# Decoder layer, cross-attention stage: longer distances between the slots' steps, side work spread over the slots, and the second layer norm applied by ACT

## The chip, the cores and the metric

One Trainium2 chip, one NeuronCore. The metric is the device time of one launch in microseconds; lower is better. PE is TensorE, DVE is VectorE, ACT is ScalarE, POOL is GpSimd, SP is SyncE, which here only issues DMAs.

## The reference, cut to what matters

64 sequences of 64 tokens, width 256, so 4,096 token rows. Three sublayers, each followed by a residual add and a layer norm without weights:

```python
x = _layernorm(x + attn(x))            # 16 heads of 128, ALiBi, causal
x = _layernorm(x + xattn(x, ctx, seg)) # the stage that is changed
x = _layernorm(x + ffn(x))             # bit-linear: activations quantised to 8 bits by row

# xattn
kv_c = kv @ W_kvc                      # 64 wide, shared by all heads
q_c = q @ W_dq                         # 96 wide
q_nope, q_rope = q_c @ W_uq, _rope(q_c @ W_qr)
k_nope, v, k_rope = kv_c @ W_uk, kv_c @ W_uv, _rope(kv_c @ W_kr)
scores = (q_nope . k_nope + q_rope . k_rope) * scale
scores = where((k_ids <= seg) & (k_ids >= seg - 8), scores, NEG)
out = softmax(scores) @ v
out @ W_o
```

The kernel folds W_uq with W_uk and W_uv with W_o beforehand, so that keys and values are the 64 latent columns of each token.

## The kernel before, in words

The layer runs as blocks: self-attention, a short start of cross-attention (`start_cross`), cross-attention, feed-forward. Each block ends when all its engines have ended. The change touches only `cross_attention` (lines 816 to 1254).

**Tiling.** The 4,096 tokens are 8 tiles of 512 tokens (8 sequences). The 16 heads are taken two at a time, so a tile has 8 slots and the stage 64 work items m. Line 865: `S_AT, T_AT, PV_AT, PROJ_AT = 3, 4, 6, 7`. In slot n = 8j + g (j the tile, g from 0 to 7) every engine runs a fixed list of steps written out by hand; a step with distance d works on item m = n - d. The loop has 82 slots: 64 with new items and 18 that drain the pipeline. Engines are not in lockstep: each runs its own list in order, and semaphores hold it where data or a buffer is missing.

**Steps of one item**, by short names that the prediction uses:

- R, L (PE, L1002 and L1006, distance 0): rotary part and latent part of the queries, three passes of bf16 high and low parts each. turn, cos (DVE, L1142 and L1156) multiply the rotary part with the tables; SP sends `x_turn` to `x_turned` with two DMAs that swap row pairs (L923); qh (DVE, L1151, distance 1) adds both; lat (ACT, L1086) copies the latent part; qhl (POOL, L793 from L1228, distance 1) makes the low part.
- S (PE, L971 and L979, distance 3): mask and scores into the one PSUM tile `xsP`. ntop (DVE, L1134): negated row maximum. exp (ACT, L1073): 8 exponentials, each with a row sum.
- inv (DVE, L1124), norm (POOL, L1215), T (PE, L1014: transposes into `xptP`), pth (ACT, L1081), all at distance 4; ptl (DVE, L1129) at distance 5.
- O (PE, L992, distance 6): probabilities times values into `xoP`. oA (ACT, L1064) copies it out; SP rearranges it with four DMAs into `oB` (L917).
- oBl (POOL) and P (PE, L1025, distance 7): low part and output projection, summed over the 8 items of a tile in `xprojP`.

**Order in one slot**, before: PE runs S, O, R, L, other, T, P. ACT runs oA, exp, copy_out, pth, lat, first layer norm (LN1), roots. DVE runs inv, ptl, ntop, residual add, turn, qh, cos, extras. POOL runs norm, oBl, qhl, extras. SP issues oB, then x_turned, then others.

**other** (L936 to L963) is one PE step a slot that also uses the PSUM tile `xoP`; what it is depends on g: transposes of x for the next tile (xt, twice), the key product (kv), the key rotation (kr), the query product (qc), the transpose of the latents (tk), and transposes of quantised rows of an earlier tile (xq, twice). It waits until oA of that slot has emptied `xoP` and until the last other was copied out. copy_out (ACT, L1035) empties `xoP` again; for kr, DVE does it (kturn, L1161), then SP moves 64 rows (moved_k, L927) and DVE adds them in slot g = 6 (kadd, L1167).

**Side work of a tile that is done**: residual add (DVE, L1138, g = 7 of the next tile), bn_stats and bn_aggr (DVE, g = 0 and 1, two tiles on), two small root steps (ACT, L1098 and L1100, g = 2), the second layer norm itself (LN2: DVE, L1182, g = 3, four instructions of 128x256), row maximum for the quantisation (DVE, L1186, g = 4), quantisation (POOL, L1247, g = 6) and its transposes xq. LN1 of the tile two ahead is applied by ACT (L601) as scale times x plus shift, in slots g = 1, 3 and 5. In the slots from 64 on, ACT and DVE also quantise the feed-forward weights (L1105, L1110, L1201, L1203).

Of the kernel before, what the change touches and what calls it, by code (L numbers as in the profile page):

```python
# [5 lines left out]
F32 = mybir.dt.float32  # L6
# [5 lines left out]
P = 128  # L12
# [4 lines left out]
TILE = 512  # L17
# [798 lines left out]
def cross_attention(nc, a, X, norm, ident, late, ffn, sem, sb, part):  # L816
# [20 lines left out]
    probs = sb("x_probs", [P, 2, PB, 2, T], F32)  # L837
# [3 lines left out]
    oBl = sb("oBl", [P, 2, TILE], BF16)  # L841
    xs = late["uqT"][:, :, :].rearrange("p h n -> p (h n)")[:, 0:PB * C].rearrange("p (b c) -> p b c", b=PB)
    stats2 = sb("ln2_stats", [P, NB, 6], F32)
# [21 lines left out]
    S_AT, T_AT, PV_AT, PROJ_AT = 3, 4, 6, 7  # L865
    LAST = N + 2 * HP + 2
# [5 lines left out]
    def step(n):  # L872


        j, g = divmod(n, HP)
        kind, c, tile = (("xq", 0, j - 3), ("xq", 1, j - 3), ("xt", 0, j + 1), ("kv", 0, j + 1),
                         ("xt", 1, j + 1), ("kr", 0, j + 1), ("qc", 0, j + 1), ("tk", 0, j + 1))[g]
        return (kind, c, tile) if 0 <= tile < NT and (kind != "xq" or n < LAST) else (None, 0, 0)

# [14 lines left out]
    with nc.Block() as block:  # L894
        @block.sync
        def _(sp):
# [12 lines left out]
            for n in range(LAST):  # L909
                j, g = divmod(n, HP)  # L910
                if has(n, PV_AT):
# [7 lines left out]
                if has(n, 0):  # L919
                    wait(sp, s_turn, n + 1)  # L920
                    wait(sp, s_qh, n - 1)
                    for h in range(2):
                        sp.dma_start(turned[1 - h::2, n % 2, :], turn[h::2, n % 2, :]).then_inc(s_swap[n % 2], 16)  # L923
                if step(n)[0] == "kr":
                    wait(sp, s_kturn, turns_before(n + 1))
                    wait(sp, s_kadd, turns_before(n))
                    sp.dma_start(moved_k[0:R, :], turned_k[R:P, :]).then_inc(s_kmoved, 16)  # L927
                if g == 4 and j + 3 < NT:
                    wait(sp, s_step, steps_before(n))
                    load_ctx(j + 3)  # L930
                if 1 <= n < 4:
                    ffn_weights(n - 1, ("wgT", "wuT", "wdT")[n - 1])

        @block.tensor
        def _(pe):
# [28 lines left out]
            for n in range(LAST):  # L964
                if has(n, S_AT):
# [14 lines left out]
                    last.then_inc(s_s, 1)  # L980
                if has(n, PV_AT):
# [13 lines left out]
                if has(n, 0):  # L995
                    tile, g = divmod(n, HP)
                    wait(pe, s_qcl, tile)
                    qc = high_part(qcf[:, tile % 2, :]), qcl[:, tile % 2, :]
                    rope_w = high_part(qr[:, g * P:(g + 1) * P]), qrl[:, g * P:(g + 1) * P]
                    wait(pe, s_qh, n - 1)  # L1000
                    for i, (u, z) in enumerate(PASSES):
                        last = nc.tensor.matmul(ropeP[n % 2][:, :], rope_w[u], qc[z], start=(i == 0), stop=(i == 2))  # L1002
                    last.then_inc(s_ropeP, 1)
                    wait(pe, s_lat, n)
                    for i, (u, z) in enumerate(PASSES):
                        last = nc.tensor.matmul(latP[:, :], WQ[:, u, g, :], qc[z], start=(i == 0), stop=(i == 2))  # L1006
                    last.then_inc(s_latP, 1)
                other(n)
                if has(n, T_AT):
                    m = n - T_AT  # L1010
                    wait(pe, s_norm, m + 1)
                    wait(pe, s_ptl, m)
                    for b in range(PB):
                        last = nc.tensor.transpose(ptP[:, b * P:(b + 1) * P], probs[:, m % 2, b].rearrange("p q s -> p (q s)"), ident[:, :])  # L1014
                    last.then_inc(s_pt, 1)
                if has(n, PROJ_AT):
# [10 lines left out]
                    last.then_inc(s_proj, 1)  # L1027
                if n == WEIGHTS_AT + 3:
                    wait(pe, late["s_abs"], 3)
                    wait(pe, s_lat, N)  # L1030
                    nc.tensor.matmul(latP[:, 0:3], kept["ones"][:, :], late["w_sums"][:, :], start=True, stop=True).then_inc(s_sum, 1)

        @block.scalar
        def _(act):
# [21 lines left out]
            LN1_BLOCKS = {1: (0,), 3: (1,), 5: (2, 3)}  # L1056

            for n in range(LAST):
                j, g = divmod(n, HP)
                if has(n, PV_AT):  # L1060
# [5 lines left out]
                if has(n, S_AT):  # L1066
                    m = n - S_AT
                    wait(act, s_top, m + 1)
                    wait(act, s_inv, m)
                    wait(act, s_pt, m - 1)  # L1070
                    for b in range(BT):
                        at_ = b % PB * 2 + b // PB
                        last = nc.scalar.activation(probs[:, m % 2, b % PB, b // PB, :], sP[:, b * T:(b + 1) * T], ACT.Exp,  # L1073
                                                    bias=ntop[:, b:b + 1], accum_out=total[:, at_:at_ + 1])
                    last.then_inc(s_exp, 1)
                copy_out(n)
# [5 lines left out]
                if has(n, 0):  # L1082
# [5 lines left out]
                    last.then_inc(s_lat, 1)  # L1088
                if j + 2 < NT and g in LN1_BLOCKS:
                    for b in LN1_BLOCKS[g]:  # L1090
                        last = norm.by_scalar((j + 2) * PB + b)
                    if g == 5:
                        last.then_inc(s_ln1, 1)
                u = j - 2
                if g == 2 and 0 <= u < NT:
                    own = slice(u * PB, (u + 1) * PB)
                    wait(act, s_mom, NB // NT * (u + 1))
                    nc.scalar.activation(rstd2[:, own], moments[:, own, 1], ACT.Ln, bias=norm.eps_col[:, :]).then_inc(s_ln, 1)  # L1098
                    wait(act, s_ln, u + 1)
                    nc.scalar.activation(rstd2[:, own], rstd2[:, own], ACT.Exp, scale=-0.5).then_inc(s_root, 1)  # L1100
# [13 lines left out]
        def _(dve):  # L1114
# [3 lines left out]
            for n in range(LAST):  # L1118
                j, g = divmod(n, HP)
                if has(n, T_AT):  # L1120
                    m = n - T_AT
# [3 lines left out]
                if has(n, T_AT + 1):  # L1125
                    m = n - T_AT - 1
# [81 lines left out]
        def _(pool):  # L1208
            for n in range(LAST):
                j, g = divmod(n, HP)  # L1210
                if has(n, T_AT):
                    m = n - T_AT
                    wait(pool, s_inv, m + 1)
                    p_ = probs[:, m % 2].rearrange("p b q s -> p (b q) s")
# [6 lines left out]
                if has(n, 1):  # L1221
                    m = n - 1
                    wait(pool, s_lat, m + 1)
                    wait(pool, s_qh, m + 1)
                    wait(pool, s_s, m - 2)
                    low_of(nc.gpsimd, qhl[:, m % 3, :], qh[:, m % 3].rearrange("p b i t -> p (b i t)")).then_inc(s_ql, 1)
                t = j + 1
                if g == 0 and 1 <= j < NT:  # L1228
                    wait(pool, s_out, outs_before(n))
# [11 lines left out]
                if g == 6 and 0 <= j - 2 < NT:  # L1241
                    u = j - 2
                    wait(pool, s_xinv, u + 1)
                    wait(pool, s_step, steps_before(HP * (u + 2) + 2) if u >= 1 else 0)
                    for b in range(PB):
                        i = u * PB + b
                        last = nc.gpsimd.tensor_scalar(xs[:, b, :], X[:, i, :], xinv[:, i:i + 1], MAGIC, ALU.mult, ALU.add)  # L1247
                    last.then_inc(s_xs, 1)
                if g == 7 and t < NT:
                    wait(pool, s_out, outs_before(n))  # L1250
                    low_of(nc.gpsimd, qcl[:, t % 2, :], qcf[:, t % 2, :]).then_inc(s_qcl, 1)
                    wait(pool, s_kadd, t)
                    wait(pool, s_s, HP * (t - 1))
                    low_of(nc.gpsimd, kl[:, t % 2, :], kf[:, t % 2, :]).then_inc(s_kl, 1)
# [225 lines left out]
```

## Time and profile before

| | |
|---|---|
| median of 3 runs | 1553.95 us (1551.09 to 1557.82) |
| the profiled execution's own time | 1553.69 us |
| its span, first to last instruction | 1551.9 us |
| mean granted TensorE clock | 0.978 |
| self-attention and start of cross-attention | 0 to about 997 us |
| cross-attention's slots | about 997 to 1421 us |
| feed-forward | about 1422 to 1552 us |
| busy over the span | PE 91%, DVE 78%, ACT 80%, POOL 79% |

One execution was traced, on the one core. A row of the timeline gives start and length of an instruction in us; a row of the windows gives how long each engine was busy in a stretch. Instructions on one engine overlap by about 0.1 us, so the distance from one start to the next start is what an instruction costs its engine, and is a little less than its length. The turn instruction of slot n on DVE (L1142) is used as the mark of a slot: a tile's length is the time from its first turn to the next tile's.

### The profile page before, as it was taken

What the parts mean: (1) busy time and instruction counts of PE and PEld (TensorE: products, weight loads), DVE (VectorE), ACT (ScalarE), POOL (GpSimd) and SP (SyncE); (2) the same over time, 40 slices, a digit from 0 to 9 for tenths busy, and PEclk for the clock granted to TensorE, in tenths of its full rate; (3) what the DMA queues carried; (4) which work ended last, traced back from release to release, by engine and by line L of the source; (5) the groups of instructions that cost most, each with busy time, mean ns of one, the idle gap of its engine ahead of it and who ended that gap; (6) DMA issues with size and microseconds to landing.
All of it is one profiled execution on the core that took longest, in us unless ns stands there. A gap on an engine that the chain in (4) does not pass through costs nothing. (4 is left out here: it accounts for less than half of the span.)

```text
span 1551.9 us, 53900 instructions
## 1 busy us (share of the span) xinstructions
PE 1411.0 (91%) x19782; PEld 1051.1 (68%) x19986; DVE 1213.6 (78%) x2852; ACT 1245.4 (80%) x4006; POOL 1231.9 (79%) x1196
## 2 busy tenths in 40 slices
PE   5898999999999999999999997789999999875997
PEld 3666777777777777777777775456666667652665
DVE  4877787777777777777777787577988889865997
ACT  5877888888888888888888886488888888873786
POOL 5899889889889888988989985377888888752565
PEclk9999999999999999999999998699999999997999
DMA  7600000000000000000000000244333333320011
GB/s 232 182 12 16 16 3 16 17 3 16 16 3 16 16 3 16 16 3 16 16 3 16 3 3 2 73 139 110 104 101 95 102 95 90 90 69 7 15 42 55
DMA packets 58370, 71.66 MB, mean 46 GB/s; under 512 B 14560, under 2 KB 42528, under 8 KB 58112
## 3 DMA queue, kind: packets, MB, share of 16 engines
q1 hardware_dynamic: 58112, 68.22, 15.1%
q8 instruction: 162, 2.65, 0.7%
q14 instruction: 96, 0.79, 0.2%
HBM read 29.39 MB, written 4.19 MB: 22 GB/s over the span
## 5 line engine op out<-in xcount | busy, mean ns | idle before, releaser
L440 DVE SCALAR_TENSOR_TENSOR X<-projP,r,X 128x256 f32<-128x256 f32 x512 | 211.2, 475 | 3.2 <-PE projP L257 3.2
L237 PEld LDWEIGHTS svP<-W,xT 128*128 128x128 bf16 x3072 | 182.2, 98 | 30.3 <-DVE scores L427 0.2
L503 POOL TENSOR_TENSOR y_sql<-y_sq 128x512 bf16<-128x512 f32 x128 | 133.0, 1039 | 78.7 <-ACT y_sq L324 78.4
L237 PE MATMUL svP<-W,xT 128*128 128x128 bf16 x3072 | 192.5, 219 | 0.0
L208 PE MATMUL qkssP<-xT,W 128*128 128x512 bf16 x641 | 161.4, 383 | 33.4 <-issue 20.3
L208 PE MATMUL kP<-xT,W 128*128 128x512 bf16 x768 | 187.0, 380 | 0.0
L257 PE MATMUL projP<-W,y 128*128 128x256 bf16 x1024 | 177.0, 275 | 3.3 <-POOL yl L503 3.2
L793 POOL TENSOR_TENSOR qhl<-qh 128x1024 bf16<-128x1024 f32 x64 | 121.2, 1893 | 65.6 <-issue 47.7
L339 ACT ACTIVATE probs<-scores,ntop 128x64 f32<-128x64 f32 x512 | 170.5, 339 | 2.1 <-DVE ntop L430 2.0
L1073 ACT ACTIVATE x_probs<-xsP,x_ntop 128x64 f32<-128x64 f32 x512 | 152.4, 332 | 14.9 <-DVE x_ntop L1134 14.6
L503 POOL TENSOR_TENSOR k_sql<-k_sq 128x512 bf16<-128x512 f32 x128 | 133.2, 1040 | 22.1 <-ACT k_sq L344 21.4
L257 PE MATMUL projP<-W,yl 128*128 128x256 bf16 x512 | 141.0, 275 | 0.0
L538 POOL TENSOR_TENSOR ql<-q 128x512 bf16<-128x512 f32 x128 | 139.4, 1089 | 0.0
L503 POOL TENSOR_TENSOR q_sql<-q_sq 128x512 bf16<-128x512 f32 x128 | 133.0, 1039 | 6.5 <-ACT q_sq L331 6.5
L208 PEld LDWEIGHTS kP<-xT,W 128*128 128x128 bf16 x768 | 75.2, 98 | 91.3 <-issue 1.0
L541 POOL TENSOR_TENSOR vl<-v 128x512 bf16<-128x512 f32 x128 | 136.4, 1065 | 0.0
L503 POOL TENSOR_TENSOR yl<-y 128x512 bf16<-128x512 f32 x128 | 133.1, 1039 | 0.0
L470 DVE TENSOR_TENSOR ptl<-pyP,pth 128x256 bf16<-128x256 f32 x128 | 54.3, 424 | 96.7 <-ACT pth L358 96.7
L208 PEld LDWEIGHTS qkssP<-xT,W 128*128 128x128 bf16 x768 | 65.0, 98 | 81.7 <-issue 12.7
L453 DVE COPY v<-svP 128x512 f32<-128x512 f32 x128 | 88.4, 690 | 38.9 <-PE svP L237 37.9
L1073 ACT ACTIVATION_READ_ACCUMULATOR x_probs<-xsP,x_ntop 128x1 f32 x512 | 115.0, 226 | 0.0
L427 DVE SCALAR_TENSOR_TENSOR scores<-svP,r,bias 128x64 f32<-128x64 f32 x512 | 110.0, 278 | 4.5
(251 smaller groups left out, 4914.5 us busy)
## 6 DMA issues: line engine op xcount, KB each, us to landing
x_turned<-x_turn SPq DMA_DIRECT2D x128, 128.0 KB, 2.1
oB<-oA SPq DMA_DIRECT2D x256, 64.0 KB, 2.0
w_stage<-in_wqkvp SPq DMA_DIRECT2D x16, 512.0 KB, 3.3
x_stage<-in_xT SPq DMA_DIRECT2D x8, 512.0 KB, 4.1
X<-in_x SPq DMA_DIRECT2D x1, 4096.0 KB, 16.9
x_stage<-in_ctxT SPq DMA_DIRECT2D x8, 512.0 KB, 4.8
out<-X SPq DMA_DIRECT2D x7, 512.0 KB, 3.0
okv<-in_L_xattn_W_o SPq DMA_DIRECT2D x1, 2048.0 KB, 11.6
```

What stands on the lines that cost most here:

```text
L208: last = nc.tensor.matmul(dst[:, :], weight(parity, u, i, c), xT[:, z, c, tok], start=(c == 0 and k == 0), stop=(c == CC - 1 and k == 2))
L237: last = nc.tensor.matmul(svP[:, b * D:(b + 1) * D], xT[:, u, c, t * TILE + b * P:t * TILE + (b + 1) * P], weight(parity, z, 2, c), start= ...
L257: last = nc.tensor.matmul(projP[:, b * C:(b + 1) * C], y_part, W[:, (j - 3) // NT % 2, z, 3 * CC * D:], start=(i == 0), stop=(i == 2))
L339: last = nc.scalar.activation(probs[:, b, :], scores[:, b, :], ACT.Exp, bias=ntop[:, b:b + 1], accum_out=total[:, b:b + 1])
L427: last = nc.vector.scalar_tensor_tensor(scores[:, b, :], svP[:, b * T:(b + 1) * T], r[:, b:b + 1], row, ALU.mult, ALU.add)
L440: last = nc.vector.scalar_tensor_tensor(acc, projP[:, b * C:(b + 1) * C], r[:, PB + b:PB + b + 1], acc, ALU.mult, ALU.add)
L453: nc.vector.tensor_copy(v[:, j % 4, :], svP[:, :]).then_inc(s_ve, 1)
L503: return nc.gpsimd.tensor_tensor(dst[:, :], src[:, :], high(src, slice(None), 0, TILE), ALU.subtract)
L538: nc.gpsimd.tensor_tensor(ql[:, j % 2, :], q[:, j % 2, :], high_of(q, j % 2), ALU.subtract).then_inc(s_ql, 1)
L541: nc.gpsimd.tensor_tensor(vl[:, j % 4, :], v[:, j % 4, :], high_of(v, j % 4), ALU.subtract).then_inc(s_vl, 1)
L793: return eng.tensor_tensor(dst, src, high_part(src), ALU.subtract)
L1073: last = nc.scalar.activation(probs[:, m % 2, b % PB, b // PB, :], sP[:, b * T:(b + 1) * T], ACT.Exp, bias=ntop[:, b:b + 1], accum_out=tot ...
```

## The change

1. Distances: norm and inv stay at 4; T and pth go to 5, ptl to 6, O and oA to 7, oBl and P to 9. `x_probs` gets a third buffer. The loop has 83 slots.
2. Order in a slot. PE: S, R, L, T, O, P, other. ACT: exp, oA, roots, pth, lat, copy_out, LN1, LN2. DVE: as before with the new distances. POOL: norm, oBl, extras, and qhl last. SP: x_turned before oB.
3. Side work: xt moves from g = 2 to g = 0 and xq from g = 0, 1 to g = 1, 2; LN1 goes one block a slot at g = 0 to 3; the residual add goes to g = 1 one tile later; statistics to g = 2 and 3; roots to g = 4; row maximum to g = 7; quantisation to g = 0; low part of the keys to g = 1 and of the values to g = 4.
4. LN2: a DVE instruction of 128x4 at g = 4 makes shift = -mean * rstd, and ACT applies `scale * x + shift` in two instructions at g = 5 and two at g = 6, in place of DVE's four at g = 3.
5. `oBl` now lies in memory that the folded weights no longer need.

```diff
-    probs = sb("x_probs", [P, 2, PB, 2, T], F32)
+    probs = sb("x_probs", [P, 3, PB, 2, T], F32)
-    S_AT, T_AT, PV_AT, PROJ_AT = 3, 4, 6, 7
-    LAST = N + 2 * HP + 2
+    S_AT, NORM_AT, T_AT, PTL_AT, PV_AT, PROJ_AT = 3, 4, 5, 6, 7, 9
+    LAST = N + 2 * HP + 3
...
-        kind, c, tile = (("xq", 0, j - 3), ("xq", 1, j - 3), ("xt", 0, j + 1), ("kv", 0, j + 1),
+        kind, c, tile = (("xt", 0, j + 1), ("xq", 0, j - 3), ("xq", 1, j - 3), ("kv", 0, j + 1),
                          ("xt", 1, j + 1), ("kr", 0, j + 1), ("qc", 0, j + 1), ("tk", 0, j + 1))[g]
...
-            LN1_BLOCKS = {1: (0,), 3: (1,), 5: (2, 3)}
+            LN1_BLOCKS = {0: (0,), 1: (1,), 2: (2,), 3: (3,)}
...
-                    wait(act, s_pt, m - 1)
+                    wait(act, s_pt, m - 2)
...
+                if g in (5, 6) and 0 <= u < NT:
+                    wait(act, s_shift2, u + 1)
+                    for i in range(u * PB + 2 * g - 10, u * PB + 2 * g - 8):
+                        x = X[:, i, :]
+                        last = nc.scalar.activation(x, x, ACT.Identity, bias=shift2[:, i:i + 1], scale=rstd2[:, i:i + 1])
+                    if g == 6:
+                        last.then_inc(s_ln2, 1)
...
-                if g == 7 and 1 <= j <= NT:
-                    acc = X[:, (j - 1) * PB:j * PB, :]
-                    wait(dve, s_proj, HP * j)
+                u = j - 2
+                if g == 1 and 0 <= u < NT:
+                    acc = X[:, u * PB:(u + 1) * PB, :]
+                    wait(dve, s_proj, HP * (u + 1))
...
-                    if g == 3:
+                    if g == 4:
                         wait(dve, s_root, u + 1)
-                        for i in range(own.start, own.stop):
-                            x = X[:, i, :]
-                            last = nc.vector.tensor_scalar(x, x, moments[:, i, 0:1], rstd2[:, i:i + 1], ALU.subtract, ALU.mult)
-                        last.then_inc(s_ln2, 1)
-                    if g == 4:
+                        nc.vector.scalar_tensor_tensor(shift2[:, own], moments[:, own, 0], -1.0, rstd2[:, own], ALU.mult, ALU.mult).then_inc(s_shift2, 1)
+                    if g == 7:
                         wait(dve, s_ln2, u + 1)
                         nc.vector.tensor_reduce(xsc[:, own], X[:, own, :], AX, ALU.max, apply_absolute_value=True).then_inc(s_max, 1)
```

## Rows read from the trace of the kernel before

**Rows 1.** Busy time by engine (us), granted clock, DMA: tiles 1, 4 and 7
```profile
1035.99:1083.56 47.57, 43.57 (x491) 31.91 (x498) 37.27 (x59) 41.84 (x178) 38.16 (x32) 1.00 0.40 105
...
1180.29:1228.61 48.32, 44.85 (x499) 32.58 (x506) 43.00 (x75) 42.42 (x176) 40.52 (x36) 1.00 0.38 102
...
1325.35:1364.14 38.79, 35.84 (x417) 26.02 (x422) 35.84 (x65) 32.66 (x142) 29.56 (x26) 1.00 0.36 97
```
**Rows 2.** Waits in tile 4: total us, times, longest us
```profile
ACT oA L1064 <- PE xoP L992: 3.7, 4, 1.7
...
ACT x_probs L1073 <- DVE x_ntop L1134: 1.8, 3, 1.1
...
PE xropeP L1002 <- POOL qcl L793: 1.0, 1, 1.0
```
**Rows 3.** Timeline of DVE, slots g = 3 and 4 of tile 4: start, length
```profile
1200.06 3.10 DVE L1182 TENSOR_SCALAR X<-X,ln_moments,ln_rstd 128x256 f32<-128x256 f32 x4
...
1204.36 0.67 DVE L1142 TENSOR_TENSOR x_turn<-xropeP,tabs 128x512 f32<-128x512 f32 x1
...
1207.21 1.22 DVE L1186 TENSOR_REDUCE xsc<-X 128x4 f32<-128x1024 f32 x1
...
1208.77 0.18 DVE L1124 RECIPROCAL x_inv<-x_total 128x8 f32<-128x8 f32 x1
...
1209.46 0.68 DVE L1134 TENSOR_REDUCE x_ntop<-xsP 128x8 f32<-128x512 f32 x1
```
**Rows 4.** Timeline of DVE and of POOL at kadd, slot g = 6 of tile 4
```profile
1218.17 1.93 DVE L1167 TENSOR_TENSOR kf<-turned_k,moved_k 64x512 f32<-64x512 f32 x1
...
1217.67 1.89 POOL L793 TENSOR_TENSOR qhl<-qh 128x1024 bf16<-128x1024 f32 x1 [0.48 <-PE xoP L812]
```
**Rows 5.** LN2 over the stage: ns min/median/max, first and last start
```profile
L1182 DVE TENSOR_SCALAR X<-X,ln_moments,ln_rstd x32: 399/403/1412, 1103.3 to 1412.3; 128x256 f32<-128x256 f32 x32
```
**Rows 6.** Timeline of ACT, slot g = 1 of tile 4
```profile
1186.03 0.31 ACT L1073 ACTIVATE x_probs<-xsP,x_ntop 128x64 f32<-128x64 f32 x1
...
1188.33 0.64 ACT L1041 ACTIVATE xqT<-xoP 128x512 bf16<-128x512 f32 x1
...
1189.29 1.22 ACT L1086 ACTIVATE qh<-xlatP 64x512 f32<-64x512 f32 x2
1190.41 0.59 ACT L601 ACTIVATE X<-X,ln_shift,ln_rstd 128x256 f32<-128x256 f32 x1
1191.01 0.60 ACT L1064 ACTIVATE oA<-xoP 128x512 f32<-128x512 f32 x1
```
**Rows 7.** Timeline at handovers: S on PE, ntop on DVE, exp on ACT
```profile
1194.72 0.38 PE L971 MATMUL xsP<-mask,identb 128*128 128x512 bf16 x1
...
1195.85 0.69 DVE L1134 TENSOR_REDUCE x_ntop<-xsP 128x8 f32<-128x512 f32 x1 [0.18 <-PE xsP L979]
...
1210.17 0.31 ACT L1073 ACTIVATE x_probs<-xsP,x_ntop 128x64 f32<-128x64 f32 x1 [0.59 <-DVE x_ntop L1134]
```
**Rows 8.** Timeline of PE: other (xq, kv, kr) and the T behind it
```profile
1186.67 0.60 PE L946 MATMUL xoP<-ident,uqT 128*128 128x128 f32 x4
...
1197.74 0.42 PE L802 MATMUL xoP<-x_stage,kvf 128*64 128x512 bf16 x1
...
1199.20 0.44 PE L1014 MATMUL xptP<-ident,x_probs 128*128 128x128 f32 x2
...
1210.10 1.12 PE L955 MATMUL xoP<-kf,wkr 64*128 64x512 f32 x2
```
**Rows 9.** The transfer moved_k, all seven: landing time, min/median/max
```profile
DMA to landing us min/median/max: 2.2/2.2/3.7
```
**Rows 10.** The drain: ACT's last exp, and DVE behind the last residual add
```profile
1381.74 0.47 ACT L1073 ACTIVATE x_probs<-xsP,x_ntop 128x64 f32<-128x64 f32 x1
...
1406.55 1.22 DVE L1201 TENSOR_SCALAR okv<-okv 128x2048 f32<-128x2048 f32 x1
...
1408.95 0.42 DVE L1174 BATCH_NORM_STATS2 ln_stats<-X 128x6 f32<-128x256 f32 x1
```

More of the change, by code:

```diff
@@ L840, in cross_attention @@
     oA, oB = sb("oA", [P, 2, 2, HT], F32), sb("oB", [P, 2, TILE], F32)
-    oBl = sb("oBl", [P, 2, TILE], BF16)
-    xs = late["uqT"][:, :, :].rearrange("p h n -> p (h n)")[:, 0:PB * C].rearrange("p (b c) -> p b c", b=PB)
-    stats2 = sb("ln2_stats", [P, NB, 6], F32)
+    spare = late["uqT"][:, :, :].rearrange("p h n -> p (h n)")
+    xs = spare[:, 0:PB * C].rearrange("p (b c) -> p b c", b=PB)
+    oBl = spare[:, PB * C:PB * C + TILE].bitcast(BF16).rearrange("p (s n) -> p s n", s=2)
+    stats2, shift2 = sb("ln2_stats", [P, NB, 6], F32), sb("ln2_shift", [P, NB], F32)
+    s_shift2 = sem("q_shift")
     moments, rstd2, xinv = sb("ln2_moments", [P, NB, 2], F32), sb("ln2_rstd", [P, NB], F32), sb("xinv", [P, NB], F32)
@@ L910, in _ @@
                 j, g = divmod(n, HP)
+                if has(n, 0):
+                    wait(sp, s_turn, n + 1)
+                    wait(sp, s_qh, n - 1)
+                    for h in range(2):
+                        sp.dma_start(turned[1 - h::2, n % 2, :], turn[h::2, n % 2, :]).then_inc(s_swap[n % 2], 16)
                 if has(n, PV_AT):
@@ L918, in _ @@
                                          oA[par * KVC:(par + 1) * KVC, m % 2, i, :]).then_inc(s_ot[m % 2], 16)
[L919 to L923, printed above, removed]
                 if step(n)[0] == "kr":
@@ L980, in _ @@
                     last.then_inc(s_s, 1)
+                if has(n, 0):
+                    tile, g = divmod(n, HP)
+                    wait(pe, s_qcl, tile)
+                    qc = high_part(qcf[:, tile % 2, :]), qcl[:, tile % 2, :]
+                    rope_w = high_part(qr[:, g * P:(g + 1) * P]), qrl[:, g * P:(g + 1) * P]
+                    wait(pe, s_qh, n - 1)
+                    for i, (u, z) in enumerate(PASSES):
+                        last = nc.tensor.matmul(ropeP[n % 2][:, :], rope_w[u], qc[z], start=(i == 0), stop=(i == 2))
+                    last.then_inc(s_ropeP, 1)
+                    wait(pe, s_lat, n)
+                    for i, (u, z) in enumerate(PASSES):
+                        last = nc.tensor.matmul(latP[:, :], WQ[:, u, g, :], qc[z], start=(i == 0), stop=(i == 2))
+                    last.then_inc(s_latP, 1)
+                if has(n, T_AT):
+                    m = n - T_AT
+                    wait(pe, s_norm, m + 1)
+                    wait(pe, s_ptl, m)
+                    for b in range(PB):
+                        last = nc.tensor.transpose(ptP[:, b * P:(b + 1) * P], probs[:, m % 3, b].rearrange("p q s -> p (q s)"), ident[:, :])
+                    last.then_inc(s_pt, 1)
                 if has(n, PV_AT):
@@ L994, in _ @@
                     last.then_inc(s_o, 1)
[L995 to L1015, printed above, removed]
                 if has(n, PROJ_AT):
@@ L1027, in _ @@
                     last.then_inc(s_proj, 1)
+                other(n)
                 if n == WEIGHTS_AT + 3:
@@ L1054, in copy_out @@
                 last.then_inc(s_out, 1)
-            LN1_BLOCKS = {1: (0,), 3: (1,), 5: (2, 3)}
+            LN1_BLOCKS = {0: (0,), 1: (1,), 2: (2,), 3: (3,)}
             for n in range(LAST):
                 j, g = divmod(n, HP)
+                if has(n, S_AT):
+                    m = n - S_AT
+                    wait(act, s_top, m + 1)
+                    wait(act, s_inv, m)
+                    wait(act, s_pt, m - 2)
+                    for b in range(BT):
+                        at_ = b % PB * 2 + b // PB
+                        last = nc.scalar.activation(probs[:, m % 3, b % PB, b // PB, :], sP[:, b * T:(b + 1) * T], ACT.Exp,
+                                                    bias=ntop[:, b:b + 1], accum_out=total[:, at_:at_ + 1])
+                    last.then_inc(s_exp, 1)
                 if has(n, PV_AT):
@@ L1065, in _ @@
                                          ACT.Copy).then_inc(s_oe, 1)
[L1066 to L1069, printed above, removed]
-                    wait(act, s_pt, m - 1)
[L1071 to L1076, printed above, removed]
+                u = j - 2
+                if g == 4 and 0 <= u < NT:
+                    own = slice(u * PB, (u + 1) * PB)
+                    wait(act, s_mom, NB // NT * (u + 1))
+                    nc.scalar.activation(rstd2[:, own], moments[:, own, 1], ACT.Ln, bias=norm.eps_col[:, :]).then_inc(s_ln, 1)
+                    wait(act, s_ln, u + 1)
+                    nc.scalar.activation(rstd2[:, own], rstd2[:, own], ACT.Exp, scale=-0.5).then_inc(s_root, 1)
                 if has(n, T_AT):
@@ L1088, in _ @@
                     last.then_inc(s_lat, 1)
+                copy_out(n)
                 if j + 2 < NT and g in LN1_BLOCKS:
@@ L1091, in _ @@
                         last = norm.by_scalar((j + 2) * PB + b)
-                    if g == 5:
+                    if g == 3:
                         last.then_inc(s_ln1, 1)
[L1094 to L1100, printed above, removed]
+                if g in (5, 6) and 0 <= u < NT:
[5 more added lines that the diff above has]
+                        last.then_inc(s_ln2, 1)
                 k = n - WEIGHTS_AT
@@ L1119, in _ @@
                 j, g = divmod(n, HP)
-                if has(n, T_AT):
-                    m = n - T_AT
+                if has(n, NORM_AT):
+                    m = n - NORM_AT
                     wait(dve, s_exp, m + 1)
@@ L1124, in _ @@
                     nc.vector.reciprocal(inv[:, :], total[:, :]).then_inc(s_inv, 1)
-                if has(n, T_AT + 1):
-                    m = n - T_AT - 1
+                if has(n, PTL_AT):
+                    m = n - PTL_AT
                     wait(dve, s_pth, m + 1)
@@ L1134, in _ @@
                     nc.vector.tensor_reduce(ntop[:, :], by_token(sP[:, :]), AX, ALU.max, negate=True).then_inc(s_top, 1)
-                if g == 7 and 1 <= j <= NT:
-                    acc = X[:, (j - 1) * PB:j * PB, :]
-                    wait(dve, s_proj, HP * j)
+                u = j - 2
+                if g == 1 and 0 <= u < NT:
+                    acc = X[:, u * PB:(u + 1) * PB, :]
+                    wait(dve, s_proj, HP * (u + 1))
                     nc.vector.tensor_tensor(acc, projP[:, :].rearrange("p (b c) -> p b c", b=PB), acc, ALU.add).then_inc(s_acc, 1)
@@ L1210, in _ @@
                 j, g = divmod(n, HP)
-                if has(n, T_AT):
-                    m = n - T_AT
+                if has(n, NORM_AT):
+                    m = n - NORM_AT
                     wait(pool, s_inv, m + 1)
-                    p_ = probs[:, m % 2].rearrange("p b q s -> p (b q) s")
+                    p_ = probs[:, m % 3].rearrange("p b q s -> p (b q) s")
                     nc.gpsimd.tensor_tensor(p_, p_, inv[:, :].unsqueeze(2).to_broadcast([P, BT, T]), ALU.mult).then_inc(s_norm, 1)
@@ L1220, in _ @@
                     low_of(nc.gpsimd, oBl[:, m % 2, :], oB[:, m % 2, :]).then_inc(s_ol, 1)
[L1221 to L1229, printed above, removed]
+                t, u = j + 1, j - 3
+                if g == 0 and 0 <= u < NT:
+                    wait(pool, s_xinv, u + 1)
+                    wait(pool, s_step, steps_before(HP * (u + 2) + 3) if u >= 1 else 0)
+                    for b in range(PB):
+                        i = u * PB + b
+                        last = nc.gpsimd.tensor_scalar(xs[:, b, :], X[:, i, :], xinv[:, i:i + 1], MAGIC, ALU.mult, ALU.add)
+                    last.then_inc(s_xs, 1)
+                if g == 1 and 1 <= j < NT:
+                    wait(pool, s_kadd, j)
+                    wait(pool, s_s, HP * (j - 1))
+                    low_of(nc.gpsimd, kl[:, j % 2, :], kf[:, j % 2, :]).then_inc(s_kl, 1)
+                if g == 4 and 1 <= j < NT:
+                    wait(pool, s_out, outs_before(HP * j))
                     wait(pool, s_o, HP * (j - 1))
@@ L1240, in _ @@
                     low_of(nc.gpsimd, xl[:, c, :], xf[:, c, :]).then_inc(s_xl, 1)
[L1241 to L1248, printed above, removed]
                 if g == 7 and t < NT:
@@ L1251, in _ @@
                     low_of(nc.gpsimd, qcl[:, t % 2, :], qcf[:, t % 2, :]).then_inc(s_qcl, 1)
-                    wait(pool, s_kadd, t)
-                    wait(pool, s_s, HP * (t - 1))
-                    low_of(nc.gpsimd, kl[:, t % 2, :], kf[:, t % 2, :]).then_inc(s_kl, 1)
+                if has(n, 1):
+                    m = n - 1
+                    wait(pool, s_lat, m + 1)
+                    wait(pool, s_qh, m + 1)
+                    wait(pool, s_s, m - 2)
+                    low_of(nc.gpsimd, qhl[:, m % 3, :], qh[:, m % 3].rearrange("p b i t -> p (b i t)")).then_inc(s_ql, 1)
 def ffn_buffers(sb):
```

7 lines of the change are left out of this document (3 added, 4 removed).

## The prediction, made before the changed kernel was run

> **What bounds the stage now.** I read the busy times by stretch first, then the waits inside one tile, then the timeline of that tile. Tiles 2 to 6 repeat to 0.1 us: from the first mark of tile 2 at 1083.56 to that of tile 7 at 1325.35 are 241.8 us, 48.36 each (tile 4 is 48.32) [rows 1]. In tile 4 no engine is full: PE is busy 44.85, DVE 43.00, ACT 42.42, POOL 40.52 [rows 1]. So the tile is bounded by engines that wait for each other while each runs its own list in order. ACT loses 3.7 us waiting for O and 1.8 for ntop; PE loses 1.0 once a tile before R, because qcl is last but one in POOL's list [rows 2]. The long stop is LN2 on DVE: four instructions that took 3.10 us together [rows 3], though the same instruction takes 0.40 in half of its runs and up to 1.41 in others [rows 5]. Behind it stand inv, ptl and ntop, and behind ntop the exponentials: one of ACT's three waits for ntop is 1.1 long [rows 2].
>
> **What one slot costs after the change.** I call t the start of exp on ACT in slot n and ask when the next exp can start. Two things set it.
>
> ACT's own list, by start-to-start distances: exp 2.30 (1186.03 to 1188.33), copy_out and pth together 0.96, lat 1.12, one block of a layer norm 0.60 [rows 6]; oA is 0.60 long with 0.1 of overlap, so 0.50. Sum 5.48 with one norm block, 4.4 bare (without copy_out and norm).
>
> The loop through `xoP`. The new order puts oA behind exp on ACT and other at the end on PE, and other waits for oA: oA ends at t + 2.30 + 0.60, other starts at t + 2.95. S follows other, from S to ntop are 1.13 [rows 7], from ntop to the exp that waits for it 0.71 (1209.46 to 1210.17) [rows 3, 7]. Loop: 4.79 + other. Other is 0.5 for xq and xt (0.60 less overlap), 1.46 for kv (1197.74 to 1199.20), as good as 1.4 for qc, which is six matmuls too, 1.12 for kr [rows 8], about 0.3 for tk.
>
> DVE, when it is late: turn to cos's end 2.85, row maximum with its two small steps 1.56, inv to ntop 0.69, ntop to exp 0.71 [rows 3, 7].
>
> By slot, the larger of them:
> g = 0, 1, 2: ACT 5.5 each (loop 5.3).
> g = 3: loop with kv, 6.25.
> g = 4: ACT with the two roots in place of a norm block, 5.5. The new shift instruction needs the roots, at t + 2.8 + 0.6, and may then stand behind POOL's qhl; I take 5.6.
> g = 5: kr ends at t + 4.07, kturn on DVE 0.6, then 0.69 and 0.71: 6.1 (ACT with two LN2 blocks and no copy_out: 5.6).
> g = 6: loop with qc 6.2; ACT 6.1; DVE with kadd of 1.93 [rows 4], which starts 0.1 before cos ends, 2.75 + 1.93 + 0.69 + 0.71 = 6.1. I take 6.2.
> g = 7: DVE with the row maximum: 2.85 + 1.56 + 0.69 + 0.71 = 5.8.
> Sum 46.45, against 48.36: **1.9 us a tile**.
>
> The shift instruction is not in the trace. Nearest row: kadd, like it with both inputs in SBUF. It starts 0.50 behind a qhl of 1.89 on POOL, and ends 0.54 after it, 1.93 long [rows 4], while turn does the same columns on twice the rows in 0.67 [rows 3]: it seems to have waited for POOL. So the bounds for shift are 0.2 (a 0.18 step on small operands [rows 3]) and 0.2 + 1.9, of which ACT's slack in g = 4 hides little. But qhl starts only behind qh, at about t + 2.15, so it ends at t + 4.05 and shift loses 0.65 at most: the slot is 5.6, not 5.5. The Trainium skill (SBUF — State Buffer, "Who interferes with whom") says that a DVE instruction with two SBUF inputs and a GpSimd instruction that reads SBUF exclude each other for the whole instruction, and that ACT never waits. By that rule shift stands behind any low-part step it meets; if it met a whole qhl, exp in g = 4 would come at t + 6.9 and each tile would be 1.3 longer, some 8 us in all. The kadd row agrees with the rule.
>
> What goes at no cost: LN1 moves are the same 0.60 blocks; T, pth, ptl, O, oBl and P wait for things now one to two slots old (norm, the DMAs into oB), so PE's stops before T and P vanish; qhl as POOL's last step has a whole slot until S needs it; x_turned goes ahead of oB on SP. moved_k is now behind four oB DMAs that wait for oA. It lands in 2.2 to 3.7 [rows 9]; kadd stands a slot later, so I take 0; if it came late, kadd and all behind it would pay. POOL's list stays at 40.5 a tile, under 46.
>
> **The sum.**
> - Fill (slots 0 to 7): 2.0, bounds 0 and 4: no O and oA yet, so no loop; qcl is earlier by a qhl, and kv finds its low parts ready.
> - Tile 1 is 47.57 [rows 1]. No xq, LN2 or maximum after: 5.5 + 5.0 + 5.0 + 6.2 + 5.3 + 6.1 + 6.2 + 5.2 = 44.5: 3.1.
> - Tiles 2 to 6: 5 x 1.9 = 9.5.
> - Tile 7, seven slots, 38.79 [rows 1]: no xt, kv, kr, qc or LN1. 4.7 bare (between ACT's 4.4 and PE's mean of 5.1), 5.4 with the residual add, 5.3, 4.7, 5.3, 5.6, 5.6 = 36.6: 2.2.
> - From 1364.14 to the last exp at 1381.74 [rows 10]: 17.6; after about 17.0: 0.6.
> - Drain: DVE's two weight steps stand between the last residual add and its statistics, 1406.55 to 1408.95 [rows 10]; afterwards they run before that add: 2.4 gained. LN2 there costs 4 x 0.60 on ACT instead of 4 x 0.40 [rows 5, 6] plus shift: 1.0 lost. Net 1.4. The longer distance (P at 9) adds a slot, but drain slots have no work that paces them; ends -2 and +3.
> Together 18.8. Less 1.2 for handovers of 0.03 (ntop's end to exp's start) that my slots leave out: 17.6. The profiled execution took 1553.69 (span 1551.9 and 1.8 around it), the median of the three runs is 1553.95: 1536.
>
> **Rivals.**
> - *PE's floor.* The loop does not close because exp and oA finish earlier than I think. Then a tile is PE's or ACT's busy time: 44.85, or 42.42 + 4 x 0.60 = 44.8. With some waits 45.2: 3.2 a tile for six, 19, and 7 elsewhere: 1527. For it: five of eight slots have only 0.2 between loop and ACT's list. Against: kv, qc and kr are long on PE by themselves. 12%.
> - *Only LN2's stop goes.* The distances change nothing since each stop of PE was absorbed anyway; what goes is the longest wait for ntop, 1.1 [rows 2], seven times: 1546. For it: the waits for O and ntop are ACT's alone and PE is at 93%. 17%.
> - *ACT becomes the bound with its waits kept* (slower). Place: oA, behind exp, with other and copy_out behind it. ACT gets 2.4 more a tile and is then at 44.8, above what any but PE has today. If its idle time stays 5.9 a tile, a tile is 50.7: 7 x 2.4 = 17 more, 1571. It decides from an idle time of 3.6 a tile on; my slots leave 1.7. The Trainium skill (Perfetto Trace Analysis, "Identifying the Most-Contended Engine") says to relieve the engine of highest occupancy first; moving work from DVE to an ACT that thereby becomes fuller than DVE was would by it make a tile 1.8 longer, some 12 us. The trace speaks against it: no engine is full, and ACT's idle time ends at PE and DVE. 8%.
> - Change and gain cancel (the drain takes one more DMA round, moved_k late): 1549. 8%.
>
> **Numbers.** Forecast 55%, its own range 1530 to 1542. The range 1529 to 1547 takes in most of the second rival and leaves out most of the first, the third and the last. About 0.5%, 7.8 us, is what a measurement of this kernel can tell from no change. Faster by more: 0.55 + 0.12 + 0.10 of the second rival = 0.77; within: 0.15; slower: 0.08.
>
> **What would show it.** Tile 4 at 46 to 47 us; its slots g = 3, 5, 6 the longest; no PE wait for qcl and almost none for oBl or norm; a new wait of PE at xt, xq and kv for oA, 0.1 to 0.3 each; ACT busy 44.8 and idle under 2; DVE busy about 40. Wrong if ACT still waits over 3 a tile, if kadd waits for moved_k, if the shift takes over 1 us, or if the drain behind the last exp (40.3 to the end of the stage) grows.

## The result, and the profile of the changed kernel

The changed kernel takes 1538.43 us, median of four runs (1537.75 to 1539.64), against 1554.8 us for the kernel before in the same comparison: a ratio of 0.9896, 95% interval 0.9876 to 0.9916. In a later comparison it took 1539.15 us, ratio 0.9879 (0.9864 to 0.9894). The profiled execution has a span of 1537.0 us against 1551.9. The prediction was 1536, in a range of 1529 to 1547.

Busy time by engine in tiles 1 and 4 after the change (columns as in [rows 1]: PE, PE's weight loads, DVE, ACT, POOL, granted clock, DMA share, GB/s):

```profile
1035.43:1080.31 44.88, 42.12 (x479) 30.69 (x486) 36.33 (x59) 40.81 (x171) 37.21 (x31) 1.00 0.41 110
1172.51:1218.95 46.44, 44.41 (x499) 32.71 (x506) 40.16 (x73) 44.04 (x178) 40.04 (x37) 1.00 0.39 107
```

A tile went from 48.32 [rows 1] to 46.44. ACT is busy for 44.04 of it and idle for 2.4, where it had been idle for 5.9; DVE fell by 2.8. Waits of that tile (total us, times, longest):

```profile
ACT x_probs L1069 <- DVE x_ntop L1143: 1.9, 3, 0.7
...
PEld xoP L952 <- ACT oA L1076: 1.1, 2, 0.8
...
DVE kf L1177 <- DMA moved_k<-turned_k: 0.5, 1, 0.5
```

ACT's wait for O (3.7 in [rows 2]) and PE's wait for qcl are gone. In their place other waits for oA, in every kind of it (xt, two waits of the weight load, is the one shown; PEld is that load), and ACT's wait for ntop stays at 1.9 (1.8 in [rows 2]).

Slot by slot, from the start of one exp to the start of the next, in tile 4 (us):

| g | 0 | 1 | 2 | 3 | 4 | 5 | 6 | 7 | sum |
|---|---|---|---|---|---|---|---|---|---|
| before | 6.85 | 5.48 | 5.51 | 7.45 | 5.71 | 5.51 | 5.84 | 5.95 | 48.3 |
| after | 5.50 | 5.49 | 5.48 | 6.32 | 5.46 | 6.15 | 6.24 | 5.78 | 46.4 |

The gain lies in two slots, g = 0 (1.35) and g = 3 (1.13), and the slots of kr and qc, g = 5 and 6, give 1.04 of it back. At g = 3 stood LN2's stop. At g = 0 the kernel before had PE wait 1.0 for qcl ahead of R, and ACT wait 1.7, its longest, for the O of the next slot [rows 2].

Where the time went, stage by stage in the two traces (us; the stage begins with the first turn; sums of the marks):

| stretch | before | after | difference | predicted |
|---|---|---|---|---|
| ahead of the stage (not touched) | 998.3 | 999.9 | +1.6 | 0 |
| tile 0 | 37.7 | 35.6 | -2.1 | -2.0 |
| tile 1 | 47.6 | 44.9 | -2.7 | -3.1 |
| tiles 2 to 6 | 241.8 | 231.6 | -10.2 | -9.5 |
| tile 7, seven slots | 38.8 | 36.3 | -2.5 | -2.2 |
| to the last exp | 17.6 | 17.2 | -0.4 | -0.6 |
| last exp to last P | 23.6 | 26.3 | +2.7 | 0 |
| last P to the stage's end | 14.7 | 13.6 | -1.1 | -1.4 |
| feed-forward (not touched) | 131.8 | 131.8 | 0 | 0 |

(The prediction takes 1.2 off the sum of its column, for handovers between engines.) A second trace of the changed kernel agrees within 0.3 in tiles 1 to 7, but its tile 0 took 37.1 in place of 35.6, at a granted clock of 0.92 in place of 0.98, and its drain 40.5 in place of 39.9.

Over all traced executions the first row lies between 993.8 and 1000.2. So below, where a few us matter, the length of the stage itself stands beside the median: 421.8 before, 405.3 and 407.6 in the changed kernel's two traces.

### The profile page after: what moved, and what is told of

It is laid out like the page before. It is cut to its first block and busy times, and to the rows that moved or that the text cites. A ratio compares the mean times of both kernels' runs of the same rounds, so it can differ in the third digit from the quotient of the medians.

```text
span 1537.0 us, 53907 instructions
## 1 busy us (share of the span) xinstructions
PE 1407.7 (92%) x19782; PEld 1053.3 (69%) x19986; DVE 1196.7 (78%) x2828; ACT 1259.5 (82%) x4038; POOL 1230.3 (80%) x1196
```

## The experiments

"Tile" is the length of tile 4. The diffs are against the changed kernel unless the text says otherwise.

**1 and 11. LN2 back on DVE.**

```diff
-        # ACT, g = 5 and 6: four ACT.Identity with shift2 and rstd2
         # DVE, g = 4
-                        nc.vector.scalar_tensor_tensor(shift2[:, own], ...)
+                        for i in range(own.start, own.stop):
+                            last = nc.vector.tensor_scalar(x, x, moments[:, i, 0:1], rstd2[:, i:i + 1], ALU.subtract, ALU.mult)
+                        last.then_inc(s_ln2, 1)
```

> The changed kernel with LN2 back on DVE (four instructions at g = 4), nothing on ACT. Slot theory: only g = 4 changes, from 5.5 to 2.85 + 0.6 + LN2 (1.6 if POOL does not stand in its way, 3.1 as in the kernel before) + 1.4 = 6.4 to 7.9, so +0.9 to +2.4 a tile; the relief of ACT brings nothing in g = 5 and 6, which wait for kr and qc. Over six tiles 5 to 14, less 2 in the drain: 1541 to 1550. Rival (the distances and the order bring all of it, LN2's place nothing): 1538. Rival (ACT's load is the bound): faster than 1538.

Measured: 1539.47 us (1536.98 to 1541.19), ratio 0.9904 (0.9888 to 0.9921). The median agrees with the rival, but the trace does not: a tile is 47.54, the distance of exps in g = 4 is 6.50 in place of 5.46, and the whole stage took 411.0, while it began at 994.0 in this execution. So both kernels were run once more, side by side.

> Repeat of the changed kernel with LN2 back on DVE, beside the changed kernel itself on the same chip. From the first trace: g = 4 takes 6.5 in place of 5.5, 1.1 a tile, so 4 to 6 slower than the changed kernel: 1543. Rival (the medians of the first job are right, no difference): 1539.

> The changed kernel unaltered, for the three beside it: 1538, a tile of 46.44, and the start of the slots anywhere between 994 and 1000, since the self-attention ahead of them differs by that between executions.

Measured: 1543.98 us (1539.02 to 1545.0), ratio 0.9904 (0.9887 to 0.992), and the changed kernel 1539.15; the stage took 412.4 against 407.6. The tile:

```profile
1176.28:1223.74 47.46, 45.49 (x507) 32.62 (x506) 41.70 (x75) 42.19 (x174) 40.03 (x37) 1.00 0.38 104
```

and LN2 on DVE in its slot g = 4, with the POOL instruction that it meets (start, length):

```profile
1201.38 1.89 POOL L793 TENSOR_TENSOR qhl<-qh 128x1024 bf16<-128x1024 f32 x1 [1.57 <-issue]
...
1202.61 1.78 DVE L1184 TENSOR_SCALAR X<-X,ln_moments,ln_rstd 128x256 f32<-128x256 f32 x4 [0.63 <-ACT ln_rstd L1084]
```

The four instructions took 1.78, not 3.10 as in [rows 3]. There the first two took 1.41 and 1.12, each until 0.15 after the end of a low-part step on POOL (qhl, then xl); here only the first meets such a step, when it is two thirds over, since the instructions wait for the roots first and xl is not in this slot. The move of LN2 is worth 1.0 us a tile, 46.5 against 47.5, in two traces; the stage differs by 3.4 to 7.0 and the medians by 1.0 and 4.8.

**2. The kernel before, with LN2 on ACT alone.**

```diff
+                if g in (3, 4) and 0 <= u < NT:   # ACT
+                        last = nc.scalar.activation(x, x, ACT.Identity, bias=shift2[:, i:i + 1], scale=rstd2[:, i:i + 1])
                     if g == 3:                    # DVE
-                            last = nc.vector.tensor_scalar(x, x, moments[:, i, 0:1], rstd2[:, i:i + 1], ALU.subtract, ALU.mult)
+                        nc.vector.scalar_tensor_tensor(shift2[:, own], ...)
-                    if g == 4:
+                    if g == 5:                    # row maximum
```

> The kernel before with LN2 on ACT (shift on DVE at g = 3, two instructions each at g = 3 and 4, row maximum at g = 5) and nothing else. Slot theory: DVE's stop of 3.1 at g = 3 goes, but ACT has 6.7 in g = 3 and 5.6 in g = 4: about 1.0 a tile gained, 1546 to 1549. Rival (LN2's stop is all that the change removes): as the changed kernel, 1538. Rival (it is all distances): 1554.

Measured: 1556.32 us, ratio 1.0014 (1.0002 to 1.0027): no gain, where I had expected 1.0 a tile. Tiles 3 to 6 took 48.1 to 48.6, tile 2 took 48.9. From one exp to the next, tile 4 has 6.54 in place of 7.45 at g = 3, but 5.98 for 5.71 at g = 4 and 6.54 for 5.84 at g = 6: with the old order the stop turns up in other slots. The rival that LN2's stop is what the change removes is out.

**3. oA ahead of exp in ACT's list.**

```diff
-                if has(n, S_AT):    # exp
                 if has(n, PV_AT):   # oA
...
+                if has(n, S_AT):    # exp
```

> The changed kernel with oA ahead of exp in ACT's list, as in the kernel before; distances and the other engines' order stay. Slot theory: O now ends 3.55 after S starts, then oA 0.5 and exp 2.5, and the next S needs xsP back: 6.5 a slot in every slot, 52 a tile, +6 a tile: about 1580. Rival (ACT's list is the bound and its order matters little): 1538 to 1542.

Measured: 1598.61 us, ratio 1.0279 (1.0262 to 1.0296). A tile is 53.66 and seven of its eight slots take 6.66 or 6.67 (expected 6.5). Its longest waits:

```profile
PE xsP L981 <- ACT x_probs L1075: 10.4, 8, 1.7
PEld xsP L973 <- POOL qhl L793: 9.7, 7, 1.6
ACT oA L1066 <- PE xoP L1014: 8.8, 8, 1.4
```

ACT waits for O and S for exp, in all eight slots: the ring of S, O, oA, exp. The order of two steps is worth 7.2 us a tile, since PE now runs O late in its slot. (The total is 18 us above the expectation: a slot is 0.16 longer than expected, and tiles 1 and 7, where side work is missing, got as long as the others or longer, 55.9 and, in seven slots, 47.0.)

**4. P at distance 8.**

```diff
-    ... PV_AT, PROJ_AT = 3, 4, 5, 6, 7, 9
+    ... PV_AT, PROJ_AT = 3, 4, 5, 6, 7, 8
-                if g == 1 and 0 <= u < NT:   # residual add
+                if g == 0 and 0 <= u < NT:
```

> The changed kernel with oBl and P at distance 8 in place of 9, and the residual add at g = 0 for it. Slot theory: the DMAs into oB land 3.9 after oA ends, 1.0 after the next slot's exp has started; oBl 1.0 more; P and other 0.5 later in each slot: +2.5 a tile, 1553 with 2 less in the drain. Rival (the longer distance of P covers nothing): 1536, a slot shorter in the drain.

Measured: 1587.0 us (1582.18 to 1596.4), ratio 1.02 (1.0167 to 1.0232): the mechanism as expected, the size about three times as large (49 us more than the changed kernel, where 15 were expected). Tiles 1 to 6 of the traced execution, the slowest of the four, take 50.4 to 56.3 and no two are alike. Part of that is PE's clock: it was granted at 0.92 in tile 1 and at 0.97 in tiles 2, 5 and 6, where the changed kernel had 1.00. Tiles 3 and 4, at 1.00, took 5.4 and 3.9 more, where 2.5 were expected. Waits in tile 4:

```profile
POOL uqT L793 <- DMA oB<-oA: 7.5, 7, 1.6
PEld xprojP L1026 <- POOL uqT L793: 5.9, 6, 1.6
```

(uqT is the memory that now holds oBl.) I had the DMAs land 1.0 after the next exp starts and POOL free to do the rest. But oBl is second in POOL's list, and POOL's timeline shows qhl and the next norm following it without a pause, so they are late too. The drain, expected 2 shorter, got longer: 32.1 from the last exp to the last P, against 26.3, at a granted clock of 0.79 against 0.91. The longer distance covers the DMAs into oB, one of the two large parts of the change that the runs isolate; the other is in experiment 3.

**9. T, ptl, O and P each one slot earlier.**

```diff
-    S_AT, NORM_AT, T_AT, PTL_AT, PV_AT, PROJ_AT = 3, 4, 5, 6, 7, 9
+    S_AT, NORM_AT, T_AT, PTL_AT, PV_AT, PROJ_AT = 3, 4, 4, 5, 6, 8
```

(and the residual add at g = 0; oA and P stay two slots apart.)

> The changed kernel with T at distance 4 again (the slot of its norm) and ptl, O, P with it at 5, 6 and 8 (the residual add at g = 0 for it); the order in the slots stays. Slot theory: norm ends on POOL about when PE comes to T, in g = 1 and 2 about 0.3 too late, which is lost in ACT's list: a tile 46.4 to 46.9, the drain a slot shorter: 1536 to 1541. Rival (the gain comes from norm being a slot old when T needs it): half of it goes, 1546.

Measured: 1540.56 us (1537.32 to 1546.45), ratio 0.9903 (0.9885 to 0.9921). A tile is 46.77, 0.33 longer, all of it in one slot (5.83 in place of 5.48 at g = 2), as expected. T's own slot of distance brings 0.3 a tile.

**5. kv and qc cut to their high parts** (four of six matmuls each left out, so keys, values and queries have bf16 precision).

```diff
-        for i, (u, z) in enumerate(PASSES):
+        for i, (u, z) in enumerate(PASSES[:1]):
...
```

> The changed kernel with kv and qc cut to two of their six matmuls (the high parts only; both low-part passes are left out). Slot theory: g = 3 falls from 6.3 to ACT's 5.5, g = 6 from 6.2 only to 6.1, where ACT's list and DVE's kadd take over: -0.9 a tile, -6 in all: 1532. Rival (PE's total work is the bound): 8 matmuls of 0.22 a tile, -1.8 a tile, -12: 1526.

Measured: 1529.59 us, ratio 0.9834 (0.9814 to 0.9854); the stage 399.0, 6.3 less than in the changed kernel's first trace. Tiles 2 to 6 take 44.8 to 45.7, on average 1.1 less each (expected 0.9; the rival said 1.8). g = 3 went from 6.32 to 5.49, which is ACT's own list; g = 6 went from 6.24 to 6.0 in three of the five tiles and to 6.2 and 6.4 in the others, as kadd and two LN2 blocks are there. PE was relieved of eight matmuls a tile, and the tile gave back about the part that the slot theory allows. The median, 1529.59, lies midway between the theory's 1532 and the rival's 1526, so here the slots decide and not the total.

**6. No LN2 at all** (ACT's 32 instructions are left out).

```diff
-                if g in (5, 6) and 0 <= u < NT:
-                        last = nc.scalar.activation(x, x, ACT.Identity, bias=shift2[:, i:i + 1], scale=rstd2[:, i:i + 1])
...
-                        wait(dve, s_ln2, u + 1)
+                        wait(dve, s_shift2, u + 1)
```

> The changed kernel without the application of LN2 (ACT's 32 instructions are left out, the shift stays). Slot theory: the tile stays at 46.4, since g = 5 and 6 wait for kr and qc and not for ACT; only the drain gets shorter by 2 to 4: 1535. Rival (ACT is the bound after the change): -2.4 a tile as well, 1520.

Measured: 1535.21 us, ratio 0.9867 (0.9843 to 0.9891). Tile 4:

```profile
1171.28:1217.71 46.43, 45.14 (x507) 32.73 (x506) 40.64 (x73) 42.08 (x174) 40.04 (x37) 1.00 0.40 107
```

ACT does 2.0 less and the tile stays at 46.43; its eight distances between exps agree with those of the changed kernel to 0.01. LN2 on ACT is free in tiles 2 to 6, because g = 5 and 6 wait for kr and qc. Shorter are only tile 7, which has no kr and qc (35.6 in place of 36.3), and the end of the drain (last P to the end 11.2 in place of 13.6). ACT is the busiest engine after PE and not the bound.

**7 and 8. The drain.** Seven moves ACT's three weight steps behind the last oA and DVE's behind them; eight also gives LN2 of the last two tiles to DVE.

```diff
-                if 4 <= k < 7:                          # ACT
+                for i in {6: (0, 1), 7: (2,)}.get(k, ()):
...
-                if 5 <= k < 8:                          # DVE
+                for i in {7: (0, 1), 8: (2,)}.get(k, ()):
...
-                if g in (5, 6) and 0 <= u < NT:         # eight only
+                if g in (5, 6) and 0 <= u < NT - 2:
...
```

> The changed kernel with ACT's three weight steps (L1119) moved behind the last oA, slots 70 and 71, and DVE's six behind them, slots 71 and 72. Theory of the drain: oA of the last items stands behind 2.1 us weight steps on ACT; without them the last P comes 4 to 7 earlier, and the weight steps fit into ACT's idle 7 us: 1532 to 1535. Rival (the chain of DMAs into oB paces the drain): 1538.

> As the run before, and LN2 of the last two tiles on DVE, which is idle in the drain. Theory: 2.2 less on ACT ahead of the last oA and 0.9 less behind the last residual add: 1530 to 1533. Rival (DMA chain): only the 0.9, 1537.

Measured: 1543.26 us, ratio 0.9919 (0.99 to 0.9938), and 1540.01 us, ratio 0.9908 (0.9888 to 0.9927). Seven is slower than the changed kernel and eight no faster, where I had expected 3 to 8 us less; both expectations failed. From the last exp to the last P there are 26.31 and 26.42, against 26.29: ACT's weight steps did not pace it. Behind the last P there are 16.7 and 14.9 against 13.6, since DVE's weight steps hold the residual add up again: in seven it starts 2.1 after the last P. My theory of the drain falls; the rival, that the DMAs into oB pace it, fits. Timeline of POOL in the drain of the changed kernel, and then what the DMA queue itself waited for, from the last turn to the last P, before and after:

```profile
1384.49 1.23 POOL L793 TENSOR_TENSOR uqT<-oB 128x512 bf16<-128x512 f32 x1 [2.22 <-DMA oB<-oA]
1387.75 1.88 POOL L793 TENSOR_TENSOR uqT<-oB 128x512 bf16<-128x512 f32 x1 [2.04 <-DMA oB<-oA]
```
```profile
SPq L42 <- PE xprojP L1025: 3.4, 2, 2.4
```
```profile
SPq L42 <- PE xprojP L1026: 11.2, 7, 3.2
```

All the last oBl wait for DMAs. By the code, the DMAs of item m also wait for P of item m - 2, as oB has two buffers. P of m - 2 used to come in the slot ahead of O of m and now comes in the same slot, and the queue waits 11.2 for P where it waited 3.4. Whether this wait is what lengthens the drain was not tried (it would take a third oB). A shorter distance does not settle it: with P one slot behind oA (experiment 4) the queue waits only 3.3 for P, but the drain is 5.8 longer. With every step from T to P one slot earlier (experiment 9) it takes 25.2 from the last exp to the last P, but the last exp comes 1.4 later.

**10. oA inside exp, and LN2 of the last two tiles on DVE** (the second edit as in experiment 8, left out below).

```diff
                     for b in range(BT):
+                        if b == 6 and has(n, PV_AT):
+                            out_of_xoP(n - PV_AT)       # oA
                         last = nc.scalar.activation(probs[...], sP[...], ACT.Exp, ...)
```

> The changed kernel with oA on ACT between the sixth and the seventh of the eight exponentials, and LN2 of the last two tiles on DVE. Slot theory: other no longer waits for oA but for PE's own list, 0.12 to 0.15 sooner: -0.4 a tile in g = 3, 5 and 6 together, the light slots unchanged (ACT's list); drain 1 to 2 less. 1533 to 1535. Rival (oA's place in exp changes nothing): 1537. Rival (oA waits for O and holds exp up, as with oA ahead of exp): above 1545.

Measured: 1533.58 us (1526.59 to 1535.32), ratio 0.9836 (0.9814 to 0.9857), against 0.9879 (0.9864 to 0.9894) for the changed kernel in the same comparison: it beats both kernels. The tile and the slot g = 3 of it, on ACT, PE and ACT:

```profile
1169.32:1214.67 45.35, 44.91 (x508) 32.72 (x507) 40.68 (x72) 43.94 (x178) 40.00 (x37) 1.00 0.41 109
```
```profile
1185.92 0.31 ACT L1077 ACTIVATE x_probs<-xsP,x_ntop 128x64 f32<-128x64 f32 x1
...
1187.65 0.62 ACT L1065 ACTIVATE oA<-xoP 128x512 f32<-128x512 f32 x1
...
1188.46 0.41 PE L802 MATMUL xoP<-x_stage,kvf 128*64 128x512 bf16 x1
...
1191.76 0.31 ACT L1077 ACTIVATE x_probs<-xsP,x_ntop 128x64 f32<-128x64 f32 x1 [0.26 <-DVE x_ntop L1147]
```

oA runs 1.73 after exp starts in place of 2.30, other starts at once behind P, and the slot takes 5.84 in place of 6.32; g = 5 takes 5.87 for 6.15, g = 6 5.99 for 6.24. No matmul waits for oA any more; two weight loads still do, for 0.3 and 0.2. Tile 4 gained 1.1 and tiles 2 to 6 on average 0.8, where I had expected 0.4. The drain as a whole did not change (40.1 against 39.9 and 40.5), though LN2 on DVE made its end about 1 shorter.

## Why the prediction was right

**The slots.** The step "the larger of ACT's list and the loop through xoP" held: every slot of tile 4 came within 0.15 us of its forecast and the tile, at 46.44, within 0.01 of 46.45. The largest miss is g = 4, 5.46 where 5.6 was taken. Slot g = 3 in the changed kernel, exp, oA, kv, exp:

```profile
1189.11 0.30 ACT L1069 ACTIVATE x_probs<-xsP,x_ntop 128x64 f32<-128x64 f32 x1
...
1191.41 0.64 ACT L1076 ACTIVATE oA<-xoP 128x512 f32<-128x512 f32 x1
...
1192.11 0.41 PE L802 MATMUL xoP<-x_stage,kvf 128*64 128x512 bf16 x1
...
1195.42 0.31 ACT L1069 ACTIVATE x_probs<-xsP,x_ntop 128x64 f32<-128x64 f32 x1 [0.68 <-DVE x_ntop L1143]
```

Other started at t + 3.00 (predicted 2.95) and the next exp came at t + 6.31 (predicted 6.25). Experiments 3, 5, 6 and 10 change one term each, and the tile follows: 3 closes another ring, 5 takes most of kv and qc out, 6 takes away ACT's work and moves nothing, 10 takes oA out of the loop.

**The shift instruction.** It lost 0.5 of the 0.65 that was priced, and slot g = 4 had the room, so it cost nothing. First as it meets qhl in tile 4, then alone in the drain:

```profile
1197.61 1.89 POOL L793 TENSOR_TENSOR qhl<-qh 128x1024 bf16<-128x1024 f32 x1 [1.56 <-issue]
```
```profile
1198.84 0.69 DVE L1189 SCALAR_TENSOR_TENSOR ln_shift<-ln_moments,ln_rstd 128x4 f32<-128x4 f32 x1 [0.62 <-ACT ln_rstd L1084]
```
```profile
1395.60 0.16 DVE L1189 SCALAR_TENSOR_TENSOR ln_shift<-ln_moments,ln_rstd 128x4 f32<-128x4 f32 x1 [0.84 <-ACT ln_rstd L1084]
```

The same instruction on four columns takes 0.16 when POOL is idle. In each of the six tiles where it met qhl it took 0.61 to 0.69 and ended 0.02 after qhl did. The Trainium skill (SBUF — State Buffer, "Who interferes with whom") says that a DVE instruction with two SBUF inputs contends with a GpSimd instruction that reads SBUF. The trace agrees, on a tiny operand too.

**moved_k.** "Wrong if kadd waits for moved_k": it did, once. moved_k landed 3.8 after its issue at worst, and kadd waited 0.5 for it in tile 4 and in no other tile. But then kadd took 1.34 in place of 1.93 and ended 0.55 after qhl, as in the tiles where it did not wait. The price of 0 was right, for a reason that I had not given.

**What was off.** The drain, predicted 1.4 shorter, was 1.5 longer, and 2.2 in the second trace; this too stood among the signs of being wrong. I took the way to the last P as unchanged, and it grew by 2.7. That step failed ("drain slots have no work that paces them"): the drain is a chain with DMAs in it. And P at distance 9 in place of 7 moves the last P by two slots, from slot 70 to slot 72, where I counted the one slot that the loop gets longer. What lengthens the drain stays open (experiments 4, 7, 8 and 9).

The 1.2 for handovers was not needed. The 2.0 for the fill came out (2.1) by luck: in the second trace tile 0 gained 0.6. The stage began 1.6 later in the traced execution, by chance. Drain +2.9, start +1.6, handovers -1.2, the stretches up to the last exp -0.6 and the time around the span +0.1 make 2.8, which is what lies between the forecast from the profiled execution (1553.69 less 17.6) and 1538.94. So the forecast of 1536 came within 3 us in part because these errors have both signs.

**The rivals.** PE's floor of 45.2 was not reached, but experiment 10 comes to 45.35 with one step moved, so the loop was what held it off, as argued. "Only LN2's stop goes" is wrong as it stands: alone the move of LN2 brings nothing (experiment 2), beside the rest it is worth 1.0 a tile, up to 6 of the 16 us. "ACT becomes the bound" is wrong (experiment 6). The Trainium skill (Perfetto Trace Analysis, "Identifying the Most-Contended Engine") says to optimize the engine of highest occupancy first. Of DVE, ACT and POOL that was DVE before the change, 43.0 of 48.3, and it was relieved; but ACT then stood at 44.0 of 46.4, above what DVE had, and the tile got shorter all the same. Taking 2.0 off ACT again gave nothing.

**The parts, by taking each away:** oA behind exp on ACT 7.2 a tile (experiment 3), distance of P 3.9 and 5.4 in the tiles at full clock and up to 11 in the others (experiment 4), LN2 1.0, T's distance 0.3. They don't add up to the gain of 1.9: oA behind exp and P at 9 are needed together with PE's new order, without either of which the kernel is slower than the one before. Not taken away by any run are POOL's new list (qcl and the other extras ahead of qhl), SP's new order and the side work's new slots. That matters, since 1.35 us a tile are gained at g = 0, where PE had waited 1.0 for qcl. That POOL's list brings this part is argued from the waits and not shown by a run.

## What to carry to other kernels

Where no engine is full, write down for each slot the list of the fullest engine and the ring of waits that returns to it, and take the larger of them by slot. Here this gave every slot of tile 4 to 0.15 us, while ACT, busy for 44.0 of 46.4, could be relieved of 2.0 for nothing. A step that frees a buffer for another engine belongs in its list as early as its input is ready, even between the pieces of a longer step (experiment 10), and not earlier (experiment 3). A longer distance pays where a DMA lies between two steps. The drain has to be priced as a chain of its own, with its DMAs and buffers.

## What the runs showed of the hardware

Three kinds of DVE instruction that met a low-part step on POOL all ended shortly after that step, whatever their size. The shift with two SBUF inputs of 128x4 took 0.69 and ended 0.02 after it, and took 0.16 alone. kadd, with two SBUF inputs of 64x512, took 1.34 or 1.93, by when it started, and ended 0.55 after it. LN2 on DVE, one SBUF input of 128x256 with two columns of scalars, took 0.75 to 1.41 when it met one and ended 0.15 after it, and took 0.40 alone.

The part ahead of the stage took 993.8 to 1000.2 us from one traced execution to another, and tile 0 of the changed kernel 35.6 and 37.1, more than some of the effects measured here. Such effects were read from marks inside the stage.
